# Attention stage with value products in two parts, the reciprocal kept in PSUM and the maximum over chunks taken by pairwise maxima

## The reference

```python
q = _qdq(x) @ _qdq(wq).T + bq
kv = cond @ wkv.T + bkv                      # cond: 32 x 1500 x 256
k, v = jnp.split(kv, 2, axis=-1)             # 16 heads of 16
attn = softmax(einsum('bnhd,bmhd->bhnm', q, k) * scale, axis=-1)
o = einsum('bhnm,bmhd->bnhd', attn, v)
out = _qdq(o) @ _qdq(wp).T + bp
```

## Time and profile before

| | us |
|---|---|
| median of 3 runs (lowest, highest) | 2720.78 (2718.15, 2728.79) |
| the profiled execution | 2719.58 |
| its span in the profile | 2717.7 |

### The profile page before, as it was taken

The page is one execution under the profiler, slowest core; times in us unless marked ns, Lnnn a source line. Parts: engine busy times, 40 slices in busy tenths (PEclk is TensorE's granted clock), DMA queues, the critical chain, the costliest instruction groups (busy, mean ns, idle before and its releaser), DMA issues. The chain is left out here.

```text
span 2717.7 us, 74884 instructions
## 1 busy us (share of the span) xinstructions
PE 2407.2 (89%) x30926; PEld 2080.7 (77%) x30926; DVE 1907.8 (70%) x2467; ACT 1493.9 (55%) x2070; POOL 1771.2 (65%) x1225
## 2 busy tenths in 40 slices
PE   5999999999899999488889888898988888859998
PEld 3999999999865665277778777777877777749998
DVE  4888888888752665657777677677767777745554
ACT  2666666666512444156666566665656666624443
POOL 2888888888614888257767667766766777722222
PEclk9999999999989999789999999999999999969999
DMA  4545454445192444211110111011011101041000
GB/s 113 180 136 157 140 156 136 158 139 156 45 282 76 134 132 137 66 47 48 48 48 25 48 48 47 26 47 48 28 45 47 48 26 47 25 150 38 8 8 14
DMA packets 92036, 224.56 MB, mean 83 GB/s; under 512 B 13589, under 2 KB 61954, under 8 KB 87778
## 3 DMA queue, kind: packets, MB, share of 16 engines
q1 hardware_dynamic: 60480, 193.17, 22.7%
q10 hardware_dynamic: 28082, 19.13, 2.3%
q0 software_dynamic: 3216, 8.29, 1.0%
HBM read 193.23 MB, written 27.33 MB: 81 GB/s over the span
## 5 line engine op out<-in xcount | busy, mean ns | idle before, releaser
L1488 POOL TENSOR_TENSOR a_ring<-a_ring,a_tops 125x1792 f32<-125x1792 f32 x128 | 513.3, 4033 | 286.0 <-ACT a_tops L1545 286.0
L1528 ACT COPY a_ring<-a_s 125x1792 f32<-125x1792 f32 x192 | 318.3, 1658 | 202.2 <-PE a_s L1703 202.2
L435 POOL TENSOR_TENSOR l_rows_lo<-l_raw,l_rows_hi 125x512 fp32r<-125x512 f32 x192 | 273.1, 1422 | 105.7 <-ACT l_rows_hi L470 105.7
L1538 ACT ACTIVATE a_ring<-a_ring 125x1792 f32<-125x1792 f32 x192 | 322.7, 1700 | 1.0 <-POOL a_ring L1488 1.0
L438 POOL TENSOR_TENSOR l_phik_lo<-l_phif,l_phik_hi 125x512 fp32r<-125x512 f32 x192 | 297.9, 1551 | 11.8 <-ACT l_phik_hi L476 11.8
L534 DVE TENSOR_TENSOR l_ctxT_lo<-l_rawT,l_ctxT_hi 128x500 fp32r<-128x500 f32 x192 | 213.5, 1112 | 95.9 <-ACT l_ctxT_hi L453 95.8
L80 PE MATMUL l_k<-T_Wk_lo,l_ctxT_hi 128*125 128x256 f32 x768 | 224.9, 293 | 36.1 <-DVE l_phif L551 26.3
L1582 DVE TENSOR_TENSOR a_val<-a_a,bv 125x512 f32<-125x512 f32 x192 | 132.1, 688 | 160.8 <-PE a_a L80 160.7
L1733 PE MATMUL a_x<-a_ring,a_val 125*17 125x56 f32 x12288 | 181.7, 218 | 68.3 <-issue 62.9
L1703 PE MATMUL a_s<-a_qbd,a_keyT 32*125 32x112 f32 x6144 | 226.7, 282 | 15.4 <-issue 10.7
L80 PE MATMUL a_a<-T_wv_lo,a_ctxT_hi 128*125 128x256 f32 x768 | 234.2, 305 | 2.5 <-issue 1.7
(11 more groups left out here) (307 smaller groups left out, 6947.2 us busy)
## 6 DMA issues: line engine op xcount, KB each, us to landing
l_rawT<-in_ctxT SPq DMA_DIRECT2D x32, 1500.0 KB, 6.2
a_rawT<-in_ctxT SPq DMA_DIRECT2D x32, 1500.0 KB, 6.2
l_raw<-in_ctx SPq DMA_DIRECT2D x32, 1344.0 KB
e_wall<-in_L_ffn_w_gate_up SPq DMA_DIRECT2D x8, 1024.0 KB, 14.0
W_hi<-e_xn ACTq DMA_DIRECT2D x32, 192.0 KB, 2.3
W_lo<-e_xn ACTq DMA_DIRECT2D x32, 192.0 KB, 3.0
l_raw<-in_ctx SPq DMA_DIRECT2D x32, 156.0 KB
e_xb<-sorted_x SPq DMA_DIRECT2D x35, 129.0 KB, 2.1
```

What stands on the lines that cost most here:

```text
L435: pool.tensor_tensor(rows.lo[:, sl, 0:D], raw[u][:, sl, :], rows.hi[:, sl, 0:D].bitcast(F32), ALU.subtract).then_inc(rows_lo, 1)
L1488: pool.tensor_tensor(now, now, tops[:, :, :].unsqueeze(2).to_broadcast([CH, 4, 4, TT]), ALU.subtract).then_inc(shifted_late, 1)
L1528: act.copy(chunks_flat(scores_of(u, k, g)), s_bank[0:CH, :, 0:TG]).then_inc(s_copied, 1)
L1538: act.activation(now, now, ACT.Exp).then_inc(exp_done, 1)
```

## The change

X is cut into its two halves of 48 products, X00 and X01 for example, each an entry of its own in the order, with another piece between them; the first half waits for each exponential only when it reaches its chunks. `a_x_full` counts twice per step. The reciprocal is written into PSUM behind the sums, and the tile `a_inv` goes. J is two operations on half the columns each: the later two chunks are joined in place in the score banks, the earlier two in `a_top`. A new entry G (`fold`) takes one maximum of two chunks into the bank `a_m` and one into `a_top`, and M becomes the maximum of these two instead of a reduction. The next step's first scores wait for G instead of J. A value copy now also waits for the products of two batches earlier. `shift` takes the group as an argument, with `SHIFTS = 1` the split between VectorE and GpSimd stays. All four orders are new.

```diff
--- before.py
+++ after.py
@@ -1201,26 +1201,27 @@
 
 
 TENSOR_ORDER = (
-    "F0' V1 V3 S10 V2 K12 T0 S11 +K00 M0 "
-    "X1' S12 V5 +K01 V4 F1' +S00 +V0 +K10 +S01 "
-    "T1 +K02 M1 X0 +S02 +K11 "
+    "+K01 M0 S11 X10' +K02 X11' S12 +K11 +K00 +V3 "
+    "F1' +V2 +S00 T1 +V5 M1 +S01 X00 +V0 X01 "
+    "+S02 +K10 +K12 F0 +V4 +V1 +S10 +T0 "
 ).split()
 SCALAR_ORDER = (
-    "K11 E10' E11' C10 E12' C11 K12 Z0 +K00 O1' "
-    "C12 E00 +K01 E01 +C00 E02 +C01 Z1 +K02 +K10 "
-    "O0 +C02 "
+    "O0' C02 K10 K12 E11' E12' C10 Z0 C11 E00 "
+    "+K01 +K02 C12 +K11 O1' +K00 E01 E02 +C00 Z1 "
+    "+C01 E10 "
 ).split()
 VECTOR_ORDER = (
-    "P0 U1' J0 V1 V3 M0 V2 D0' R0 P1 "
-    "U0 V5 J1 V4 D1' M1 +V0 R1 "
+    "R0 D0' U00 P1 J1 G1 M1 +V3 +V2 R1 "
+    "D1' U10 +P0 +V5 +V0 +J0 +G0 +M0 +V4 +V1 "
 ).split()
 GPSIMD_ORDER = (
-    "C1 U01' U02' C2 Q1 U11' U12' +Q0 +C0 "
+    "U02' Q1 +C1 U11' U12' +Q0 +C2 +C0 U01 "
 ).split()
 
 GW = S // KG
 HALF = KG
 RING, TURN = 8, 4
+SHIFTS = 1
 
 
 def turns(order, b, u=0):
@@ -1388,7 +1389,7 @@
         ring = c.sb("a_ring", [CH, RING, 4, 4, TT])
         top, most = c.sb("a_top", [CH, 4, 4, TT]), c.sb("a_most", [CH, 4, TT])
         mx, tops = c.sb("a_mx", [TT, 4]), c.sb("a_tops", [CH, 4, TT])
-        outs, inv = c.sb("a_outs", [P, TT]), c.sb("a_inv", [P, TT])
+        outs = c.sb("a_outs", [P, TT])
         one = c.sb("a_one", [P, 2])
         gated_bias, bias_gated = c.sb("a_gated_bias", [TT, D]), c.sem("a_bias_gated")
         s_bank = c.ps("a_s", [P, 4, 512])
@@ -1400,13 +1401,14 @@
         a_full, a_read = each("a_full", 2), each("a_read", 2)
         s_full, s_copied = c.sem("a_s_full"), c.sem("a_s_copied")
         paired, joined, most_done = c.sem("a_paired"), c.sem("a_joined"), c.sem("a_most_done")
+        joined_late, folded = c.sem("a_joined_late"), c.sem("a_folded")
         t_full, mx_done, m_full = c.sem("a_t_full"), c.sem("a_mx_done"), c.sem("a_m_full")
         tops_kept, shifted, shifted_late = c.sem("a_tops_kept"), c.sem("a_shifted"), c.sem("a_shifted_late")
         exp_done, x_full, x_kept = c.sem("a_exp"), c.sem("a_x_full"), c.sem("a_x_kept")
         sums_full, inv_done, out_done = c.sem("a_sums_full"), c.sem("a_inv_done"), c.sem("a_out_done")
         ones_set, masks_set = c.sem("a_ones_set"), c.sem("a_masks_set")
         x_cleared = c.sem("a_x_cleared")
-        sums_at = slice(256, 256 + TT)
+        sums_at, inv_at = slice(256, 256 + TT), 256 + TT
         block = ctx.enter_context(nc.Block())
 
         def wait(eng, sem, value):
@@ -1524,16 +1526,16 @@
                 act.wait_ge(s_full, HALF * n + g + 1)
                 freed = n + (KG + g - RING) // KG
                 if not isinstance(freed, int) or freed > 0:
-                    act.wait_ge(x_full, freed)
+                    act.wait_ge(x_full, 2 * freed)
                 act.copy(chunks_flat(scores_of(u, k, g)), s_bank[0:CH, :, 0:TG]).then_inc(s_copied, 1)
 
             def exp(b, u, k, g):
 
                 n = KC * b + k
-                if g == 0:
-                    act.wait_ge(shifted, n + 1)
+                if g < SHIFTS:
+                    act.wait_ge(shifted, SHIFTS * n + g + 1)
                 else:
-                    act.wait_ge(shifted_late, (KG - 1) * n + g)
+                    act.wait_ge(shifted_late, (KG - SHIFTS) * n + g - SHIFTS + 1)
                 now = chunks_flat(scores_of(u, k, g))
                 act.activation(now, now, ACT.Exp).then_inc(exp_done, 1)
 
@@ -1541,13 +1543,13 @@
 
                 n = KC * b + k
                 act.wait_ge(m_full, n + 1)
-                wait(act, shifted_late, (KG - 1) * n)
+                wait(act, shifted_late, (KG - SHIFTS) * n)
                 act.copy(tops[:, :, :], m_bank[0:CH, 0:TG].rearrange("p (j n) -> p j n", j=4)).then_inc(tops_kept, 1)
 
             def keep(b, k):
 
                 n = KC * b + k
-                act.wait_ge(x_full, n + 1)
+                act.wait_ge(x_full, 2 * (n + 1))
                 wait(act, out_done, 2 * n)
                 act.copy(outs[:, :], x_bank[:, 0:TT]).then_inc(x_kept, 1)
 
@@ -1578,6 +1580,7 @@
 
                 i, g = PIECE_BANK[w], int(w[1])
                 wait_piece(dve, a_full, w, b)
+                wait(dve, x_full, 2 * KC * (b - 1))
                 split_heads = lambda t: t.rearrange("p c (h e) -> p c h e", h=H)
                 dve.tensor_tensor(val[u % 2][:, g * CP:(g + 1) * CP, :, 0:HD],
                                   split_heads(a_bank[i][0:CH, :].rearrange("p (c d) -> p c d", c=CP)),
@@ -1595,15 +1598,27 @@
                 n = KC * b + k
                 dve.wait_ge(paired, n + 1)
                 dve.wait_ge(s_copied, HALF * (n + 1))
-                flat = chunks_flat(top[:, :, :, :])
-                dve.tensor_tensor(flat, s_bank[0:CH, :, 0:TG], flat, ALU.max).then_inc(joined, 1)
+                late = s_bank[0:CH, :, 2 * TT:TG]
+                dve.tensor_tensor(late, late, chunks_flat(top[:, :, 2:4, :]), ALU.max).then_inc(joined_late, 1)
+                early = chunks_flat(top[:, :, 0:2, :])
+                dve.tensor_tensor(early, s_bank[0:CH, :, 0:2 * TT], early, ALU.max).then_inc(joined, 1)
+
+            def fold(b, k):
+
+                n = KC * b + k
+                dve.wait_ge(joined_late, n + 1)
+                dve.wait_ge(joined, n + 1)
+                wait(dve, shifted, SHIFTS * n)
+                wait(dve, tops_kept, n)
+                dve.tensor_tensor(m_bank[0:CH, 0:TG].rearrange("p (j n) -> p j n", j=4), s_bank[0:CH, :, 3 * TT:TG], top[:, :, 1, :], ALU.max).then_inc(folded, 1)
+                dve.tensor_tensor(top[:, :, 0, :], s_bank[0:CH, :, 2 * TT:3 * TT], top[:, :, 0, :], ALU.max).then_inc(folded, 1)
 
             def maximum(b, k):
 
                 n = KC * b + k
-                dve.wait_ge(joined, n + 1)
+                dve.wait_ge(folded, 2 * (n + 1))
                 wait(dve, t_full, n)
-                dve.tensor_reduce(most[:, :, :], top[:, :, :, :].rearrange("p j c n -> p j n c"), AX.X, ALU.max).then_inc(most_done, 1)
+                dve.tensor_tensor(most[:, :, :], m_bank[0:CH, 0:TG].rearrange("p (j n) -> p j n", j=4), top[:, :, 0, :], ALU.max).then_inc(most_done, 1)
 
             def row_maximum(b, k):
 
@@ -1612,10 +1627,10 @@
                 wait(dve, m_full, n)
                 dve.tensor_reduce(mx[:, :], m_bank[0:TT, 0:4 * CH].rearrange("p (j n) -> p j n", j=4), AX.X, ALU.max).then_inc(mx_done, 1)
 
-            def shift(b, u, k):
+            def shift(b, u, k, g):
 
                 dve.wait_ge(tops_kept, KC * b + k + 1)
-                now = scores_of(u, k, 0)
+                now = scores_of(u, k, g)
                 dve.tensor_tensor(now, now, m_bank[0:CH, 0:TG].rearrange("p (j n) -> p j n", j=4).unsqueeze(2).to_broadcast([CH, 4, 4, TT]),
                                   ALU.subtract).then_inc(shifted, 1)
 
@@ -1623,11 +1638,11 @@
 
                 n = KC * b + k
                 dve.wait_ge(sums_full, n + 1)
-                dve.reciprocal(inv[:, :], x_bank[:, sums_at]).then_inc(inv_done, 1)
+                dve.reciprocal(x_bank[:, inv_at:inv_at + TT], x_bank[:, sums_at]).then_inc(inv_done, 1)
                 dve.wait_ge(inv_done, n + 1)
                 for r, to in enumerate((K["attT"], K["odd"])):
                     at = slice(r * L, (r + 1) * L)
-                    dve.tensor_tensor(to[:, k, bass.ds(b * L, L)], outs[:, at], inv[:, at], ALU.mult).then_inc(out_done, 1)
+                    dve.tensor_tensor(to[:, k, bass.ds(b * L, L)], outs[:, at], x_bank[:, inv_at + r * L:inv_at + (r + 1) * L], ALU.mult).then_inc(out_done, 1)
 
             def batch(b, u):
                 for w, of, at in turns(VECTOR_ORDER, b, u):
@@ -1637,12 +1652,14 @@
                         pair(of, at, int(w[1]))
                     elif w[0] == "J":
                         join(of, int(w[1]))
+                    elif w[0] == "G":
+                        fold(of, int(w[1]))
                     elif w[0] == "M":
                         maximum(of, int(w[1]))
                     elif w[0] == "R":
                         row_maximum(of, int(w[1]))
                     elif w[0] == "U":
-                        shift(of, at, int(w[1]))
+                        shift(of, at, int(w[1]), int(w[2]))
                     elif w[0] == "D":
                         outputs(of, int(w[1]))
 
@@ -1690,7 +1707,7 @@
                 n = KC * b + k
                 if g == 0:
                     pe.wait_ge(q_made[k], b + 1)
-                    wait(pe, joined, n)
+                    wait(pe, folded, 2 * n)
                 else:
                     pe.wait_ge(s_copied, HALF * n + g)
                     if g == 2:
@@ -1708,7 +1725,7 @@
 
                 n = KC * b + k
                 pe.wait_ge(most_done, n + 1)
-                wait(pe, shifted, n)
+                wait(pe, shifted, SHIFTS * n)
                 for j in range(4):
```

(23 more changed lines are left out.)

## The result

The changed kernel takes 2572.66 us (median of 4 runs, 2570.93 to 2575.23), against 2719.47 for the kernel before on the same chip: a ratio of 0.9454 (0.943 to 0.9478), 147 us less. The forecast was 2599, with its own range from 2570. The profiled execution took 2570.93, its span is 2568.9.

A forecast was written before the change was run, and what follows sets the result against it. TensorE was taken to bound the kernel. Per turn 6.8 (issue gaps) + 6.6 (T wait) - 1.0 (P before S) + 3.8 (clock) = 16.2 us; over 7.4 turns 120, giving 2599. Own range 2570 to 2635, whole range 2555 to 2675.

The forecast's parts named there:

- The bound: TensorE bounds the attention stage's steady part, needing 32.2 us of work per batch, 128.8 per turn.
- X in halves: Splitting X lets instruction fetch keep up: issue gaps fall from 12.2 to 5.4 us per turn, 6.8 saved.
- the edges: Packet boundaries at an outer edge of an X pair still cost gaps: 1.6 us per turn.
- The maximum: On VectorE, halves of J take 1.09 us, G's two and M 0.62 each, at 1.04 ns per element, PSUM included.
- rival D: Maxima that write PSUM are slow, 1.88 ns per element: 19 us slower, 2739; chance 0.05.
- The reciprocal: With one input in PSUM the multiply into attT takes 0.2 us; 0 to 0.8 saved per step, within the T wait.
- The hand-laid orders: Every wait closes in a hand-laid batch, smallest slack 0.3 us; the T wait goes, 6.6 saved per turn.
- P before S: P may come late for the S that waits for it; 1.0 us per turn left for it.
- The clock and the rest: Of about 6.3 us per turn lost to TensorE's clock, 3.8 saved, bounds 0 and 5.5; 2.4 of small gaps stay.
- The number of turns: The steady part of 1155 us is 7.4 turns; nothing counted for filling and draining, +-5 us.
- Rival A: X's issue gaps stay, belonging to X and not to the fetch: 53 us saved, 2667; chance 0.15.
- Rival B: The new order has an unseen wait of about 2 us per batch: 46 us saved, 2674; chance 0.12.

The follow-up runs named there:

- the fastest kernel: The changed kernel with TensorE's loop written out and the context load issued behind X11: 2515.15 us, ratio 0.9241 against the kernel before.
- the three edits in the old orders: The kernel before, in its old orders, with X's halves apart, the reciprocal in PSUM and the pairwise maxima: 2719.24 us, ratio 0.9986.

## Why the prediction was right, and where it was off

1. The bound. TensorE at 32.2 us of work per batch, the rest idle or clock: right; the fastest kernel shows 31.8. No other engine became the bound.
2. X in halves. The cause was right, shown by moving the halves both ways and by the edges of 256. Forecast were 5.4 us of issue gaps per turn; measured are 41.1 us in 980, 5.8 per turn. Inside it sizes are off against each other, so that the sum is nearer than its parts by luck: the load beside X10 and X11 was put at 0.9 per turn, while moving it away took 2.7 of gaps and 4.4 in all; the edges were put at 1.6 and with the load away are about 1.0; the branch was put at 2.9 and is 2.3, for there are six in 7.1 turns. The 227 records to a packet came from dividing TensorE's matmul and load records by the packets of all engines; the edges show 256, which X eats in 1.8 us and not in 1.6.
3. The maximum. 1.04 ns per element with PSUM as the target: right, 1099 and 632 ns against 1.09 and 0.62. The bound of 1.88 (rival D) is excluded. That rival was also priced too high: its 2.8 us per step take 1.88 for all five operations of the chain, and only two of them write PSUM, 1344 elements, which is 1.1 us.
4. The reciprocal. 0.2 for the multiply: right. Its worth lies within the T wait, as said, but in the new order it is nothing. The operation that it waited for was misread, the split and not the subtractions.
5. The hand-laid orders. VectorE's timeline of one batch, whose K01 starts at 1682.94:

```profile
1693.04 1.10 DVE L1602 TENSOR_TENSOR a_s<-a_s,a_top 125x896 f32<-125x896 f32 x1 [3.22 <-ACT a_ring L1530]
1694.05 1.08 DVE L1604 TENSOR_TENSOR a_top<-a_s,a_top 125x896 f32<-125x896 f32 x1
1695.22 0.63 DVE L1613 TENSOR_TENSOR a_m<-a_s,a_top 125x448 f32<-125x448 f32 x1
1695.76 0.61 DVE L1614 TENSOR_TENSOR a_top<-a_s,a_top 125x448 f32<-125x448 f32 x1
```

J1 starts at 10.1 and G1 ends at 13.4; the forecast had the last score copy, which J1 waits for, end at 10.2 and G1 at 13.65. S00 follows at 14.3, forecast 14.45. Every wait closed, the T wait is 0, and the 1.0 us per turn kept for P before S was not used.
6. The clock and the rest. 8.7 per turn lay between TensorE's need with its gaps and the period; 137.8 - 128.8 - 5.8 leaves 3.2. So 5.5 went, not 3.8, at the upper bound of 5.5: the term most off in the sum of a turn. 6.6 + 6.4 + 5.5 = 18.5 against 16.2.
7. The number of turns. I multiplied by 7.4, the length of the steady part. But the batches outside the loop gain as well: 32 batches are 8.0 turns, and 8.0 x 18.5 = 148, the measured difference of the spans (148.8). In the traces 112.4 us of it lie between the first and the last of the loop's seven branch instructions, 15.1 ahead of them and 21 behind. With 16.2 x 8.0 the forecast would have been 2590.

Rival A fell with the edges of 256. For X the rule that crossing a block is mostly hidden (the Trainium skill, "Runtime: NRT & Kernel Launch", Instruction fetch mechanics) does not hold. Its sizes hold, 256 instructions to a block, and a taken branch costs a fetch, and most edges of a turn do show no gap, but in an undivided X a block is eaten in 1.8 us and the fetch takes about 3.1. The measurement decides. Rival B did not appear in the changed kernel; it is what happened to the three edits in the old orders.

## What to carry to other kernels

Where an engine's row of short instructions has gaps put down to nothing, count records between them: gaps that keep one remainder by 256 and move when instructions are added in front are fetch, and slow instructions between the fast ones, a written-out loop and bulk loads issued at another time each take a share of them. An edit that shortens one wait is worth what the next wait leaves: lay every engine's order against the bound engine's time before the edit, and move the orders with it. Where a small VectorE operation with both inputs in SBUF ends just behind a GpSimd operation again and again, take one input from PSUM or move the operation out of GpSimd's time. And sum the waits before giving them the whole gain: part of a change can lie in the granted clock.

## What the runs showed of the hardware that I had not expected

- A bulk load doubled the time of an instruction fetch, from some 3.1 to 6.5 us, though its packet is 16 KB: the packet went 4.1 us after the edge instead of 1.1. Moving one load per batch by some 3 to 6 us was worth 30 us.
- 64 idle instructions in front of the program went with 24 us, 0.9 of the 3.8 per turn in gaps and the rest with a lower granted clock. A comparison of two kernels can carry that much chance whenever TensorE's instruction count changes: the 42 us of the reduction's return (24 records more in front of the loop's first branch) and the change itself included.
- The multiply of 0.2 us took up to 2.32, ending 71 to 75 ns behind a GpSimd operation each time, and 0.21 every time once one input was in PSUM.
